# Four-layer graph network on one core: hi and lo halves of three turned stages share one buffer and one transposing DMA

## What is computed

```python
h = relu(layernorm(x)); x = x + L0(h, adj)   # graph attention, 128 features, beside h @ W
h = relu(layernorm(x)); x = x + L1(h, adj)   # deg * (h @ Wi.T + b) + adj @ (h @ Wj.T)
h = relu(layernorm(x)); x = x + L2(h, adj)   # 8 heads: q, k, v = h @ W.T + b; masked softmax; out @ Wo.T + bo
h = relu(layernorm(x)); x = x + L3(h, adj)   # graph attention: Wh = h @ W, softmax(leaky(e_src + e_dst)) @ Wh
```

## Time and profile before

| | |
|---|---|
| median of three runs | 1322.18 us (1316.64 to 1323.46) |
| profiled execution, its own time | 1312.74 us |
| span of its trace | 1310.9 us |
| busy: PE / DVE / ACT / POOL | 88% / 80% / 76% / 71% of the span |
| granted TensorE clock, mean of the execution | 0.972 of full speed; 1.00 between 100 and 1200 us |
| DMA issues by SP: six 4-block turns, two 16-block turns, a load and a store | 64 groups each |

### The profile page before, as it was taken

The page is one execution under the profiler, slowest core; times in us unless marked ns, Lnnn a source line. Parts: engine busy times, 40 slices in busy tenths (PEclk is TensorE's granted clock), DMA queues, the critical chain, the costliest instruction groups (busy, mean ns, idle before and its releaser), DMA issues.

```text
span 1310.9 us, 39708 instructions
## 1 busy us (share of the span) xinstructions
PE 1158.1 (88%) x15385; PEld 967.8 (74%) x15385; DVE 1052.9 (80%) x2913; ACT 1001.4 (76%) x2824; POOL 936.7 (71%) x1606
## 2 busy tenths in 40 slices
PE   3578999999998999999999999998999998999855
PEld 3467878777877877787777877777878787777743
DVE  3468888888887988898888888888888888888752
ACT  2367888888878878887887888778888887888752
POOL 1357777877776777777778777877787777778540
PEclk7699999999999999999999999999999999999996
DMA  5025766665776666677656766666677556776652
GB/s 178 9 50 106 122 106 123 130 132 117 129 132 115 123 130 131 123 126 131 134 116 128 133 124 124 130 130 121 124 130 138 122 123 128 127 123 122 126 111 51
DMA packets 514492, 156.56 MB, mean 119 GB/s; under 512 B 478208, under 2 KB 514304, under 8 KB 514304
## 3 DMA queue, kind: packets, MB, share of 16 engines
q1 hardware_dynamic: 514304, 154.03, 61.6%
HBM read 19.73 MB, written 16.78 MB: 28 GB/s over the span
## 4 chain that ended last, share of the span: by engine, by line
PE 25%; ACT 19%; DVE 17%; DMA 16%; SPq 16%; POOL 5%; issue 3%; POOLq 0%; DVEq 0%
DMA h_lo<-h_rows_lo 9%; PE ps L405 5%; PE ps L407 5%; PE ps L406 5%; SPq L362 5%; DMA h_hi<-h_rows_hi 5%; SPq L346 5%; SPq L366 4%; ACT head_prob L1066 4%; ACT head_prob L1058 4%; ACT head_prob L1074 4%; DVE h_rows_lo L912 3%; DVE key_lo L850 2%; DVE head_nmax L865 2%; ACT out_rows_hi L1089 2%
## 5 line engine op out<-in xcount | busy, mean ns | idle before, releaser
L405 PE MATMUL ps<-w_hi,h_hi 128*128 128x256 f16 (+1 forms) x512 | 142.3, 278 | 35.2 <-DMA h_hi<-h_rows_hi 34.9
L406 PE MATMUL ps<-w_lo,h_hi 128*128 128x256 f16 (+1 forms) x512 | 141.6, 277 | 0.0
L407 PE MATMUL ps<-w_hi,h_lo 128*128 128x256 f16 (+1 forms) x512 | 141.5, 276 | 0.0
L406 PE MATMUL ps<-h_lo,w_hi 128*128 128x256 f16 x512 | 140.5, 274 | 0.0
L407 PE MATMUL ps<-h_hi,w_lo 128*128 128x256 f16 x512 | 140.5, 274 | 0.0
L405 PE MATMUL ps<-h_hi,w_hi 128*128 128x256 f16 x512 | 140.5, 274 | 0.0
L405 PE MATMUL ps<-w_hi,agg_hi 128*128 128x256 f16 x512 | 139.8, 273 | 0.0
L406 PE MATMUL ps<-w_lo,agg_hi 128*128 128x256 f16 x512 | 139.3, 272 | 0.0
L407 PE MATMUL ps<-w_hi,agg_lo 128*128 128x256 f16 x512 | 139.1, 272 | 0.0
L1223 POOL TENSOR_TENSOR head_lo<-head_prob,head_hi 128x512 f16<-128x512 f32 x64 | 74.1, 1157 | 85.1 <-ACT head_hi L1085 85.1
L1183 POOL TENSOR_TENSOR x<-x,g 128x256 f32<-128x256 f32 x64 | 44.5, 695 | 110.0 <-ACT g L992 110.0
(11 more groups left out here) (192 smaller groups left out, 5037.7 us busy)
## 6 DMA issues: line engine op xcount, KB each, us to landing
x<-in_x SPq DMA_DIRECT2D x64, 256.0 KB, 3.0
out<-x SPq DMA_DIRECT2D x64, 256.0 KB, 2.6
h_hi<-h_rows_hi SPq DMA_TRANSPOSE x128, 2.5
h_lo<-h_rows_lo SPq DMA_TRANSPOSE x128, 2.5
head_t_hi<-head_hi SPq DMA_TRANSPOSE x64, 5.6
head_t_lo<-head_lo SPq DMA_TRANSPOSE x64, 4.4
out_hi<-out_rows_hi SPq DMA_TRANSPOSE x64, 2.5
out_lo<-out_rows_lo SPq DMA_TRANSPOSE x64, 2.5
```

The costliest lines, as they stand in the source:

```text
L405: pe.matmul(o, lh, rh, start=start, stop=False)
L406: pe.matmul(o, lh, rl, start=False, stop=False)
L407: return pe.matmul(o, ll, rh, start=False, stop=stop)
```

## The change

`h2_rows`, `mix_rows` and `h3_rows` take the place of the pairs of hi and lo tensors: 128 x 2 x 2 x 256 fp16 each, with the hi half in [:, 0] and the lo half in [:, 1]. The turned tensors `h2_t`, `mix_t` and `h3_t` hold eight blocks, hi in the first four and lo in the last four. Each pair of DMAs becomes one DMA of eight blocks, which waits for the lo half, and stands where the lo half's stood (for h3 the lo half stood first). Each pair of semaphores becomes one, and PE waits for that one. ACT, DVE and POOL run the same instructions in the same order on the same shapes; PE runs the same matmuls.

```diff
-            def move_hi2(g):
-                sp.wait_ge(rows_hi2_done, g + 1)
-                sp.dma_start(h2_hi[g % 2][:, :, :], h2_rows_hi[g % 2][:, :, :].rearrange("p b d -> p (b d)"), transpose=True).then_inc(move_hi2_done[g % 2], 16)
-
-            def move_lo2(g):
+            def move2(g):
                 sp.wait_ge(rows_lo2_done, g + 1)
-                sp.dma_start(h2_lo[g % 2][:, :, :], h2_rows_lo[g % 2][:, :, :].rearrange("p b d -> p (b d)"), transpose=True).then_inc(move_lo2_done[g % 2], 16)
+                sp.dma_start(h2_t[g % 2][:, :, :], h2_rows[g % 2][:, :, :, :].rearrange("p h b d -> p (h b d)"), transpose=True).then_inc(move2_done[g % 2], 16)
...
             def slot(at):
-                at(6, move_lo3)
-                at(6, move_hi3)
+                at(6, move3)
                 at(0, load_x)
-                at(5, move_out_hi)
-                at(5, move_out_lo)
-                at(3, move_hi2)
-                at(3, move_lo2)
+                at(5, move_out)
+                at(3, move2)
                 at(7, store_x)
                 at(4, move_heads_hi)
                 at(4, move_heads_lo)
...
-                pe.wait_ge(move_hi2_done[g % 2], 16 * (g // 2) + 16)
-                pe.wait_ge(move_lo2_done[g % 2], 16 * (g // 2) + 16)
+                pe.wait_ge(move2_done[g % 2], 16 * (g // 2) + 16)
```

## The result

| | before | after |
|---|---|---|
| median of the timed runs | 1321.39 us (4 runs) | 1303.28 us (4 runs, 1302.06 to 1309.55) |
| ratio, 95% interval | | 0.9877 (0.9836 to 0.9919) |
| profiled execution / its span | 1312.74 / 1310.9 us | 1303.47 / 1301.7 us |

The change makes the kernel 1.2% faster, some 16 to 18 us, where 44 had been forecast. The sign was right, the size was wrong by more than half, and the time lies inside the range.

A forecast was written before the change was run, and what follows sets the result against it. The prediction took a slot-to-slot loop through PE, other engines and SP's queue to bound the kernel. 63 slots x 0.70 us = 44 us off 1322.2 gave 1278 us, range 1254 to 1318.

The forecast's parts named there:

- The reading of what bounded the kernel: Whole kernel: a loop from slot to slot, partly through PE, partly through other engines and SP's queue; mean slot 18.87 us.
- The costs of the parts: Merged turns of h2, head outputs and h3: 0.90 us gained at h2, net nothing at outputs, h3's 34.9 us wait gone.
- L: Time from issue of an eight-block turn to its landing, not in the trace; taken as 3.1 us, range 2.5 to 4.4.
- the straight line: Interpolation between four-block and sixteen-block flights, putting eight blocks a third of the way: 3.0, 3.1 or 3.5 us.
- The wait at `make_query`: PE's wait for h2's turn at the slot's start, claimed to fall from 41 us to under 15.
- Other engines: ACT, DVE and POOL run the same instructions; loop through DVE closes at 17.72 us, slot 17.73 against 18.62, gain 0.89.
- What is late next: The heads' lo-half turn at `head_sum_1`: 0.3 us of slack left, new waits where the turn needs up to 6.1 us.
- 0.70 us per slot: Gain kept of the 0.89 us per slot, after a new wait and longer slots; over 63 slots 44 us.
- Another loop takes over early: Rival: heads' lo half, POOL and ACT, or L near 3.5 limits the gain to 0.35 us per slot; 1300 us, chance 0.22.
- All three waits vanish: Rival: PE's three waits for turned tensors go, nothing new comes, 84.7 us less; 1237 us, chance 0.05.
- Slower: Rival: eight-block turn takes 4.4 us like sixteen, PE starts `make_query` 0.40 us later per slot; 1347 us, chance 0.08.
- The rule on early issue: Issue a DMA early, wait late; alone it priced the merge at 0.6 us per slot, 38 us, 1360; coalescing rule preferred.

The follow-up runs named there:

- e2: Kernel before, with one of POOL's four head splits (split_head_0) left out from group 1 on; 1316.75 us, ratio 0.9985.
- e12: Changed kernel with 13 one-column matmuls per slot on PE, and 58 more once ahead of the first slot; 1291.90 us, ratio 0.9806.
- e8: Changed kernel with empty SP instructions that never reached the core, so a second measurement of the same program; 1299.19 us, ratio 0.9835.
- e13: e11 with the matmul padding of e12 added; 1250.46 us, ratio 0.9491.
- e11: Changed kernel with one head split moved from POOL to DVE, plus three small reorderings on ACT, POOL and DVE; 1262.71 us, ratio 0.9563.
- e3: Changed kernel with ACT's expo3_0 moved ahead of rows_hi3; 1300.16 us, ratio 0.9865.
- e10: Changed kernel with 13 one-column matmuls per slot added on PE; 1337.91 us, ratio 1.0133.
- e4: Kernel before with only h2's two turns merged; 1296.79 us, ratio 0.9845.
- e7: Changed kernel with h2 in two turns again, outputs and h3 still merged; 1294.16 us, ratio 0.9800.
- e1: Changed kernel with one of POOL's four head splits (split_head_0) left out from group 1 on; 1276.75 us, ratio 0.9684.
- e9: Changed kernel with six one-column matmuls per slot added on PE; 1293.49 us, ratio 0.9797.

## Why the prediction was right or wrong

**The reading of what bounded the kernel** was right for the kernel before: e2 shows that POOL was worth nothing there, and SP's share of the chain went from 16% to 1%.

**The costs of the parts** were right. L was taken as 3.1 us and is 3.1 in the median (3.0 for the outputs), between the rows for four and for sixteen blocks as the straight line said. The issue of eight blocks is 1.23 to 1.24 us in the median, less than the 1.3 to 1.6 assumed. `move2` starts 0.03 us after DVE's end. One slip of the sum changes nothing: from landing to PE it is 0.14 us in the rows, not 0.12. The wait at `make_query` was to fall under 15 us and fell from 41.1 to 22.0, in 17 waits, 15 of them right behind a late turn; e12, with 3 late ones, has 3.1. The wait at `feat3_0` nearly went (7.6 us), as said; that at `project_0` stayed small (5.4 us, where up to 15 had been allowed), and the one forecast at `head_sum_1`, 5 to 20 us, didn't come (2.4 us).

**The step that failed** is "Other engines": the loop through DVE was taken as 14.62 + L = 17.72 us, and "What is late next" named only the heads' lo turn, with 0.3 us of slack. "ACT, DVE and POOL do the same instructions" was taken to mean that none of their loops could become the longest. The heads' turn was no limit (2.4 us of waiting, once). The ring through POOL was missed, since I had followed one path from `make_query` to the end of h2's lo half and assumed that its length would not change. It contains a place where two paths join: DVE's L912, the lo half of h3. The timeline of ACT in the kernel before has the row that decides:

```profile
655.36 0.63 ACT L1093 ACTIVATE h_rows_hi<-xn 128x512 f16<-128x512 f32 x1 [0.69 <-POOL xn L1250]
```

ACT ends this at 655.99, and DVE began L912 at 656.20. So DVE waited for its own queue there, and the arm through POOL was ready only 0.21 us earlier: the slot of 18.62 could shrink only to 18.4 before POOL's arm decided. In the steady state (200 to 1200 us) DVE waited there 10 times in the kernel before, and 42 times in the changed one; the first row is of before, the second of after:

```profile
DVE h_rows_lo L912 <- ACT h_rows_hi L1093: 2.5, 10, 0.3
```

```profile
DVE h_rows L889 <- ACT h_rows L1070: 28.1, 42, 0.8
```

**The term of the sum that was mis-sized** is the 0.70 us per slot. The median slot went from 18.67 to 18.48, by 0.19, which is the slack of 0.2 us just found; for a short slot 17.73 had been worked out. The mean went from 18.93 to 18.75, by 0.18. So 0.52 us are missing in the mean, most of it by the ring, which holds even a slot without any lateness at 18.46. On top of the ring the changed kernel lies 0.27 in the mean above its median, and two things add to it: the late landings, and the 14 slots in which `norm2_1` takes 0.54 us longer. e8, the same program without the latter, has a mean of 18.63, and e12, with hardly a late landing and its padding in the ring, 18.60. With the ring shortened and the fetches moved (e13, with the small moves of e11) the slot is 17.93 in the mean, 1.00 below that of before, where the forecast wanted 0.70. No pair of runs splits the 0.52 exactly.

**The rivals.** "Another loop takes over early" came true, with POOL and ACT behind it as it said, at 1303 against its 1300; it should have been the likeliest case. The condition given for it, 0.3 us of slack at the heads' turn, was the wrong one. "All three waits vanish" is answered by e3 and by the change itself: 49.7 of the 84.7 us went and the time fell by 16 to 18. "Slower" from L = 4.0 on was right as a mechanism: e10 holds L at 4.4 and takes 1338 us, where 1347 was worked out; its turns of h3 are late too, which that sum didn't have.

**The rule on early issue** (the Trainium skill, DMA: Bandwidth & Descriptors, Rules for kernel authors) was rightly weighed against the coalescing rule: e4 and e7, each with one part merged, are both faster than before, by 1.5% and 2.0%.

## What to carry to other kernels

In a software pipeline over in-order queues, the length of a slot is that of its longest ring. Before pricing the removal of one ring's delay, follow every joint of that ring and note by how much the other arm was late: the smallest of these slacks caps the gain, and here it was 0.2 us of 18.6. A wait of the busiest engine is no such cap and no promise: one of 41 us was removed for nothing (e3). And a chain that names a new engine after a change is best tested by the same cut in both kernels, as in e1 and e2.

## What the runs showed of the hardware

In the changed kernel an eight-block turn (128 x 1024 fp16) lands 3.1 us after its issue where one of four blocks took 2.5 before and one of sixteen takes 4.3 to 4.6, and its issue holds SP for 1.23 us, hardly more than the 1.20 of four blocks.

PE's instructions come through the same DMA engines, in packets of 256 (1.98 MB in 121 packets; 1664 more matmuls and loads in e10 make it 128). A packet that starts 1.0 to 2.1 us after the issue of an eight-block turn of h2 made it land late in all 13 cases of the changed kernel, at 4.1 to 4.7 us in place of 3.1; one that starts 2.4 to 2.7 us after it did not in any of six. The number of PE instructions in a slot therefore sets how often this happens: at 1.90 packets per slot it wanders through with a period of 10 slots, at 1.94 (e9, worked out) with 18, and at 2.00 it stays where it is, for 46 us of loss in the wrong place (e10 against e12). Why the engines stand idle for 1 us in such a flight, the runs don't show.

One POOL instruction of 128 x 256, `norm2_1`, took 1.06 us or 1.60 us beside the same two DVE instructions, with 0.06 us of difference in when the second of these began; it costs 0.54 us of slot each time.
